# Chunks summed and rounded in pairs, x_lo on GpSimd, y kept in PSUM: a conditioned FFN in split fp32

## What is computed

```python
q_emb = relu(cond @ W3 + b3)                     # one row of 512 per batch
v_sum = sum(x, axis=1, keepdims=True)            # over the 64 tokens of a batch
x1 = (64 * x + v_sum) * q_emb[:, None, :]
y = relu(x1 @ W2 + b2)
base = y @ W_base + b_base
shared = (y @ A_s) @ B_s                         # rank 16
gates = softmax(y @ W_router + b_router)         # 6 experts, the top 2 are kept
routed = sum over e of ((y @ A_r[e]) * w[e]) @ B_r[e]  # w: kept gates, not renormalised
out = x + base + shared + routed
```

## Time and profile before

| | |
|---|---|
| time, median of 3 | 252.19 us |
| the three runs | 253.6, 252.19, 251.87 us |
| span of the profiled execution | 249.2 us |
| mean granted clock of TensorE | 0.979 of full speed |
| TensorE busy | 234.5 us (94%), 999 matmuls |
| VectorE busy | 205.4 us (82%), 396 instructions |
| ScalarE busy | 90.8 us (36%), 170 instructions |
| GpSimd busy | 54.8 us (22%), 52 instructions |
| DMA | 28.47 MB, mean 114 GB/s |

### The profile page before, as it was taken

How to read it: one execution, slowest core, us unless ns; L and a number is a source line. 1 busy time by engine, 2 the same in 40 slices (tenths; PEclk the granted TensorE clock), 3 DMA queues, 4 the chain that set the end, 5 groups by cost and what they waited for, 6 DMA issues and landing times.

```text
span 249.2 us, 3161 instructions
## 1 busy us (share of the span) xinstructions
PE 234.5 (94%) x999; PEld 186.3 (75%) x999; DVE 205.4 (82%) x396; ACT 90.8 (36%) x170; POOL 54.8 (22%) x52
## 2 busy tenths in 40 slices
PE   6699799699998988999999999999999999999994
PEld 2488568478786766888888888888888888888863
DVE  0697999979998998989988997989798997752384
...
GB/s 157 291 203 208 261 231 2 170 0 291 50 3 166 0 259 187 61 1 180 194 134 0 60 277 166 6 0 257 80 0 0 168 169 0 0 60 109 3 0 168
DMA packets 32217, 28.47 MB, mean 114 GB/s; under 512 B 6173, under 2 KB 22621, under 8 KB 32206
## 3 DMA queue, kind: packets, MB, share of 16 engines
...
...
HBM read 19.94 MB, written 8.39 MB: 114 GB/s over the span
## 4 chain that ended last, share of the span: by engine, by line
PE 56%; DVE 27%; SPq 6%; DMA 4%; issue 4%; ACT 2%; POOL 1%; POOLq 0%; DVEq 0%; ACTq 0%
PE m_ps L630 51%; PE hT L630 6%; DVE xT L388 5%; DMA x_quart<-in_x_dram 4%; DVE gatesT L488 4%; DVE vsum L393 3%; DVE x_sum L402 3%; DVE x_lo L410 3%; DVE y_lo L416 3%; DVE out_nat L513 2%; SPq L212 2%; SPq L200 1%; DVE hw_full L497 1%; DVE logit L448 1%; SPq L206 1%
## 5 line engine op out<-in xcount | busy, mean ns | idle before, releaser
L267 POOL TENSOR_TENSOR x_full<-x_sum,qT 128x512 f32<-128x512 f32 x31 | 38.1, 1230 | 141.6 <-DVE x_sum L402 141.6
L630 PE MATMUL m_ps<-Wb_hi,y_hi 128*128 128x512 f32 x128 | 49.9, 390 | 0.0
L630 PE MATMUL m_ps<-Wb_lo,y_hi 128*128 128x512 f32 x128 | 49.8, 389 | 0.0
L630 PE MATMUL m_ps<-Wb_hi,y_lo 128*128 128x512 f32 x128 | 49.8, 389 | 0.0
L630 PE MATMUL m_ps<-x_hi,W_hi 128*128 128x512 f32 x112 | 44.1, 394 | 4.1 <-DVE x_lo L410 2.9
L630 PE MATMUL m_ps<-x_lo,W_hi 128*128 128x512 f32 x112 | 43.7, 390 | 0.0
L630 PE MATMUL m_ps<-x_hi,W_lo 128*128 128x512 f32 x112 | 43.6, 389 | 0.0
L388 DVE STREAM_TRANSPOSE xT<-x_quart 128x512 f32<-128x512 f32 x32 | 35.0, 1093 | 6.9 <-DMA x_quart<-in_x_dram 6.9
L312 ACT ACTIVATE y_full<-m_ps,b_sb 128x512 f32<-128x512 f32 x32 | 22.0, 688 | 40.3 <-PE m_ps L630 37.4
L304 ACT ACTIVATE x_hi<-x_full 128x512 fp32r<-128x512 f32 x32 | 20.0, 629 | 35.8 <-POOL x_full L267 35.8
L488 DVE STREAM_TRANSPOSE gatesT<-w_nat 32x128 f32<-32x128 f32 x96 | 29.1, 303 | 3.0
...
## 6 DMA issues: line engine op xcount, KB each, us to landing
...
```

Of the source, the lines that this page charges most:

```text
L267: nc.gpsimd.tensor_tensor(per_batch(x1_full[:, c, :]), per_batch(x1_sum[:, c, :]), qT[:, c, bass.ds(BG * g, BG)].unsqueeze(2).to_broadcast ...
L630: mm = nc.tensor.matmul(psum, lhsT, rhs, start=start and i == 0, stop=stop and i == len(terms) - 1)
```

## The change

- `xT` and `vsum` hold two chunks. From group 1 on, `sum_x` and `add_sum` work on a pair of chunks in one instruction (1,024 columns), and `x1_split` rounds a pair in one. `scale` still works on one chunk. Group 0 goes by single chunks (`sum_first`, `add_first`, `rest_first`).
- From group 1 on, x1_lo is made by GpSimd (`x1_rest`), after the pair was rounded, in the order scale, scale, rest, rest for each pair. TensorE also waits for x1_hi.
- ScalarE makes y_hi first and then writes relu over the bank of m1 itself; y_full is gone, and with it the wait for y_lo ahead of the relu. VectorE's `y_rest` takes y from PSUM.
- The orders on VectorE and ScalarE are rewritten accordingly; both transposes of a pair come together, and the 12 gate transposes are in one piece in all groups but the last.

```diff
-        xT = [sb(f"xT{i}", [P, TG]) for i in range(2)]
+        xT = [sb(f"xT{i}", [P, 2, TG]) for i in range(2)]
         out_nat = [sb(f"out_nat{i}", [P, TT, D]) for i in range(2)]
-        vsum = [sb(f"vsum{i}", [P, BG]) for i in range(2)]
+        vsum = [sb(f"vsum{i}", [P, 2, BG]) for i in range(2)]
         x1_sum = sb("x1_sum", [P, KC, TG])
         x1_full = sb("x1_full", [P, KC, TG])
         x1_hi = [sb(f"x1_hi{i}", [P, KC, TG], F32R) for i in range(2)]
         x1_lo = [sb(f"x1_lo{i}", [P, KC, TG], F32R) for i in range(2)]
-        y_full = [sb(f"y_full{i}", [P, TG]) for i in range(2)]
         y_hi = sb("y_hi", [P, KC, TG], F32R)
...
+
+        def pairs_done(g, j):
+
+            return KC + PAIRS * (g - 1) + j + 1
...
-                pool.wait_ge(x1_sum_ready, n + 1)
-
-                if not (isinstance(g, int) and g == 0):
+                if isinstance(g, int) and g == 0:
+                    pool.wait_ge(x1_sum_ready, c + 1)
+                else:
+                    pool.wait_ge(x1_sum_ready, pairs_done(g, c // 2))
                     pool.wait_ge(x1_lo_ready, n + 1 - KC)
                 nc.gpsimd.tensor_tensor(per_batch(x1_full[:, c, :]), per_batch(x1_sum[:, c, :]),
                                         qT[:, c, bass.ds(BG * g, BG)].unsqueeze(2).to_broadcast([P, BG, N]),
                                         ALU.mult).then_inc(x1_full_ready, 1)
+
+            def x1_rest(g, par, c):
+
+                pool.wait_ge(x1_hi_ready, pairs_done(g, c // 2))
+                nc.gpsimd.tensor_tensor(x1_lo[par][:, c, :], x1_full[:, c, :],
+                                        x1_hi[par][:, c, :].bitcast(F32), ALU.subtract).then_inc(x1_lo_ready, 1)
 
             def W_rest(lo, full, hi, n, ready):
 
@@ -281,14 +293,20 @@
             W_rest(Wd_lo[:, :, :], Wd_f[:, :, :], Wd_hi[:, :, :], KC + 1, Wd_lo_ready)
             for k in range(KC):
                 W_rest(Wb_lo[:, k, :], Wb_f[:, k, :], Wb_hi[:, k, :], KC + 2 + k, Wb_lo_ready)
-            scale(1, 0)
-            scale(1, 1)
-            W_rest(Wu_lo[:, :], Wu_f[:, :], Wu_hi[:, :], 2 * KC + 2, Wu_lo_ready)
-            for c in range(2, KC):
-                scale(1, c)
-            with pool.Fori(2, NG) as g:
-                for c in range(KC):
-                    scale(g, c)
+            def prepare(g, par, between=None):
+
+                for j in range(PAIRS):
+                    scale(g, 2 * j)
+                    scale(g, 2 * j + 1)
+                    if j == 0 and between is not None:
+                        between()
+                    x1_rest(g, par, 2 * j)
+                    x1_rest(g, par, 2 * j + 1)
+
+            prepare(1, 1, lambda: W_rest(Wu_lo[:, :], Wu_f[:, :], Wu_hi[:, :], 2 * KC + 2, Wu_lo_ready))
+            with pool.Fori(0, (NG - 2) // 2) as pair:
+                for half in range(2):
+                    prepare(pair * 2 + (2 + half), half)
 
         @block.scalar
...
-            def x1_split(g, par, c):
-
-                act.wait_ge(x1_full_ready, KC * g + c + 1)
-                nc.scalar.activation(x1_hi[par][:, c, :], x1_full[:, c, :], ACT.Copy).then_inc(x1_hi_ready, 1)
-
-            def relu(g, m, first):
+            def x1_split(g, par, c, n=1):
+
+                act.wait_ge(x1_full_ready, KC * g + c + n)
+                nc.scalar.activation(x1_hi[par][:, c:c + n, :], x1_full[:, c:c + n, :], ACT.Copy).then_inc(x1_hi_ready, 1)
+
+            def relu(g, m):
 
                 n = KC * g + m
                 act.wait_ge(m1_done, n + 1)
-                if not (first and m < 2):
-                    act.wait_ge(y_lo_ready, n - 1)
-                nc.scalar.activation(y_full[m % 2][:, :], m1_ps[m][:, :], ACT.Relu,
-                                     bias=b2_sb[:, m:m + 1]).then_inc(y_full_ready, 1)
                 nc.scalar.activation(y_hi[:, m, :], m1_ps[m][:, :], ACT.Relu,
                                      bias=b2_sb[:, m:m + 1]).then_inc(y_hi_ready, 1)
+                nc.scalar.activation(m1_ps[m][:, :], m1_ps[m][:, :], ACT.Relu,
+                                     bias=b2_sb[:, m:m + 1]).then_inc(y_full_ready, 1)
 
             act.wait_ge(condT_done, 1)
             nc.scalar.activation(condT[:, :, :], hT[:, 0:QC * B].rearrange("p (k b) -> p k b", b=B), ACT.Copy).then_inc(condT_copied, 1)
...
-                def split(c):
+                def split(j):
                     if not last:
-                        x1_split(g + 1, 1 - par, c)
+                        x1_split(g + 1, 1 - par, 2 * j, 2)
 
                 for m in range(KC):
-                    relu(g, m, first)
-                    if not first and m >= (2 if second else 1):
-                        split(m - (2 if second else 1))
+                    relu(g, m)
+                    if not first and m == (3 if second else 1):
+                        split(0)
                 if first:
                     act.wait_ge(Wu_loaded, 48)
                     nc.scalar.activation(Wu_hi[:, :], Wu_f[:, :], ACT.Copy).then_inc(W_hi_ready, 1)
@@ -361,14 +377,9 @@
                 nc.scalar.activation(h_sb[:, :], hT[:, :], ACT.Identity, bias=h_bias[:, 0:1]).then_inc(h_ready, 1)
                 if first:
                     split(0)
-                    split(1)
-                if second:
-                    split(2)
                 act.wait_ge(logit_ready, g + 1)
                 nc.scalar.activation(expo[:, :, :], logit[:, :, :], ACT.Exp).then_inc(expo_ready, 1)
-                if first:
-                    split(2)
-                split(3)
+                split(1)
                 parts = 2 if last else 1
                 for i in range(parts):
                     toks = slice(i * TG // parts, (i + 1) * TG // parts)
...
-                nc.vector.transpose(xT[c % 2][:, :], x_quart[par][:, :, :].rearrange("p b (i c) -> p c b i", c=KC)[:, c]).then_inc(xT_ready, 1)
-
-            def sum_x(g, c):
-
-                dve.wait_ge(xT_ready, KC * g + c + 1)
-                nc.vector.tensor_reduce(vsum[c % 2][:, :], per_batch(xT[c % 2][:, :]), AX.X,
+                nc.vector.transpose(xT[c // 2][:, c % 2, :], x_quart[par][:, :, :].rearrange("p b (i c) -> p c b i", c=KC)[:, c]).then_inc(xT_ready, 1)
+
+            def per_pair(ap):
+                return ap.rearrange("p c (b n) -> p (c b) n", n=N)
+
+            def sum_x(g, j):
+
+                dve.wait_ge(xT_ready, KC * g + 2 * j + 2)
+                nc.vector.tensor_reduce(vsum[j][:, :, :].rearrange("p c b -> p (c b)"), per_pair(xT[j][:, :, :]), AX.X,
                                         ALU.add).then_inc(vsum_ready, 1)
 
-            def add_sum(g, c):
-
-                n = KC * g + c
-                dve.wait_ge(vsum_ready, n + 1)
-                if not (isinstance(g, int) and g == 0):
-                    dve.wait_ge(x1_full_ready, n + 1 - KC)
+            def add_sum(g, j):
+
+                dve.wait_ge(vsum_ready, pairs_done(g, j))
+                dve.wait_ge(x1_full_ready, KC * g + 2 * j + 2 - KC)
                 nc.vector.scalar_tensor_tensor(
-                    out=per_batch(x1_sum[:, c, :]), in0=per_batch(xT[c % 2][:, :]), scalar=float(N),
-                    in1=vsum[c % 2][:, :].unsqueeze(2).to_broadcast([P, BG, N]),
+                    out=per_pair(x1_sum[:, 2 * j:2 * j + 2, :]), in0=per_pair(xT[j][:, :, :]), scalar=float(N),
+                    in1=vsum[j][:, :, :].rearrange("p c b -> p (c b)").unsqueeze(2).to_broadcast([P, 2 * BG, N]),
                     op0=ALU.mult, op1=ALU.add).then_inc(x1_sum_ready, 1)
 
-            def x1_rest(g, par, c):
-
-                dve.wait_ge(x1_hi_ready, KC * g + c + 1)
-                nc.vector.tensor_tensor(x1_lo[par][:, c, :], x1_full[:, c, :],
-                                        x1_hi[par][:, c, :].bitcast(F32), ALU.subtract).then_inc(x1_lo_ready, 1)
+            def sum_first(c):
+
+                dve.wait_ge(xT_ready, c + 1)
...
-                dve.wait_ge(y_hi_ready, KC * g + m + 1)
-                nc.vector.tensor_tensor(y_lo[:, m, :], y_full[m % 2][:, :],
+                dve.wait_ge(y_full_ready, KC * g + m + 1)
+                nc.vector.tensor_tensor(y_lo[:, m, :], m1_ps[m][:, :],
                                         y_hi[:, m, :].bitcast(F32), ALU.subtract).then_inc(y_lo_ready, 1)
 
 
             turn_x(0, 0, 0)
-            sum_x(0, 0)
...
-                def total(*chunks):
-                    for c in () if last else chunks:
-                        sum_x(g + 1, c)
-                        add_sum(g + 1, c)
-
-                def rest(*chunks):
-                    for c in () if last else chunks:
-                        x1_rest(g + 1, 1 - par, c)
+                def sums(j):
+                    if not last:
+                        sum_x(g + 1, j)
+
+                def adds(j):
+                    if not last:
+                        add_sum(g + 1, j)
 
                 if first:
-                    turn(0)
-                    total(0)
+                    turn(0, 1)
```

(94 more changed lines are left out.)

## The result

The changed kernel takes 256.16 us (median of 4 runs, 255.37 to 256.73), against 252.03 (median of 4) before: ratio 1.017, 95% interval 1.012 to 1.022. It is slower by 4.1 us. I had forecast 253.5, in a range from 251.0 to 257.0, with 0.57 on a change within 1% and 0.36 on slower. So the likeliest class did not come; the sign of the sum (+1.3) and the range held, and two thirds of the size was missed.

What follows compares the result with a forecast made beforehand. TensorE was taken to bound the kernel, losing time only in groups 0 to 2. Span 249.2 + 1.3 = 250.5, the loop adding 0 to 0.1 per group; with 3.0 between span and median, 253.5 us, range 251.0 to 257.0.

Steps and rivals of the forecast that it cites:

- the sum (+1.3): Group 2's last y_lo product at 97.45 against 96.11, so the span grows by 1.3 us; the loop adds 0 to 0.1 per group.
- (a): Loop, groups 3 to 6: turns to VectorE's pace, m1's last column tile waiting for out_nat; 255.5 us; chance 0.23.
- (b): y_lo from PSUM is blocked by GpSimd all the same; group 0's last y_lo product at 35.75, not 33.05; 256.2 us; chance 0.10.
- x_lo at 1.59 us: Upper bound for one x_lo on GpSimd, against 1.29 taken; six in the two chains, +1.8 us.
- TensorE sets the pace; only groups 0 to 2 matter: Groups 3 to 7 follow at TensorE's pace, 27.20 us; its lost time is seven waits in groups 0 to 2, 6.61 us.
- Prices: Estimated instruction times: 1024-column pair 1.23 us on VectorE, 1.06 on ScalarE; x_lo on GpSimd 1.29; y_lo from PSUM at most 0.69.
- Group 0: Group 0's y_lo products start at 28.16 to 33.05, the last having stood at 35.18: 2.13 us earlier.
- no y_lo wait over 0.2: Sign that the walk is right: TensorE has no y_lo wait of over 0.2 us in group 0.
- The chains of groups 1 and 2: Scalings, pair split and x_lo delay chunk 3's first product: 49.76 against 49.22 in group 1, 81.94 against 77.94 in group 2.
- Rival (c): GpSimd's chain is not late, so no product waits and all of 6.6 us goes: 245.6 us; chance 0.07.
- 68 products (15.4 us) and 0.1 for a restart lead to 97.45: Group 2: from chunk 3's product at 81.94, TensorE reaches the last y_lo product at 97.45, against 96.11.
- Rival (d): VectorE's pairs cost as much as two singles: +0.6 us, 254.1; chance 0.56 together with the main walk.

Runs made afterwards that it cites:

- e1_warm: Changed kernel, with TensorE running 16 products of a zero tile in groups 1 and 2 during the wait for chunk 2's x_lo: 252.45 us, ratio 1.002.
- e5_single: Changed kernel's y in PSUM and x_lo on GpSimd, but every chunk summed, scaled and rounded singly in the earlier kernel's order: 248.03 us, ratio 0.983.
- e4_psum: Kernel before plus one part of the change alone: y_hi first, relu over the bank, y_lo from PSUM: 249.13 us, ratio 0.990.

## Why the prediction was right or wrong

**The range held by luck.** Its upper part was made of (a), (b) and x_lo at 1.59 us, and none of these came; what filled it was a term that the sum did not have.

**TensorE sets the pace; only groups 0 to 2 matter: right.** The loop's groups take 27.20 us in both kernels and the rest after 100.98 is unchanged.

**Prices: right.** The groups of the changed kernel (busy, mean ns of one, idle before):

```profile
L280 POOL TENSOR_TENSOR x_lo<-x_full,x_hi 128x512 fp32r<-128x512 f32 x28 | 36.4, 1320 | 19.3 <-ACT x_hi L322 19.3
...
L442 DVE TENSOR_TENSOR y_lo<-m_ps,y_hi 128x512 fp32r<-128x512 f32 x32 | 21.8, 684 | 13.5 <-ACT m_ps L330 13.5
...
L330 ACT ACTIVATE m_ps<-m_ps,b_sb 128x512 f32<-128x512 f32 x32 | 20.9, 655 | 0.0
...
L407 DVE TENSOR_REDUCE vsum<-xT 128x16 f32<-128x1024 f32 x14 | 17.1, 1219 | 0.4
...
L322 ACT ACTIVATE x_hi<-x_full 128x1024 fp32r<-128x1024 f32 x14 | 14.8, 1054 | 35.4 <-POOL x_full L273 35.4
```

x_lo on GpSimd 1.32 us (1.29 taken), the pair sum 1.22 (1.23), the pair's rounding 1.05 (1.06), y_lo from PSUM 0.684, the relu into PSUM 0.655. The 62 cycles more for a PSUM source that the Trainium skill, VectorE: DVE Perf Modes, the errata section, charges do not appear: y_lo is no slower than the 0.693 of the SBUF form.

**y_lo from PSUM is not blocked, x_sum is: right,** rival (b) out. GpSimd's Wb_lo against two instructions of VectorE:

```profile
25.48 6.01 POOL L286 TENSOR_TENSOR Wb_lo<-Wb_f,Wb_hi 128x512 fp32r<-128x512 f32 x4
...
26.31 0.69 DVE L442 TENSOR_TENSOR y_lo<-m_ps,y_hi 128x512 fp32r<-128x512 f32 x1
...
28.64 1.72 DVE L414 SCALAR_TENSOR_TENSOR x_sum<-xT,vsum 128x1024 f32<-128x1024 f32 x1
```

At 26.31, inside GpSimd's row, y_lo takes 0.69; at 28.64 the pair addition takes 1.72 instead of 1.23. The rule of the Trainium skill, SBUF — State Buffer, Who interferes with whom, that an instruction of VectorE with at most one SBUF input does not contend, holds here for this form.

**Group 0: right in the main.** The last y_lo product is at 32.52. Its first h product came 0.9 us earlier than before by itself (26.82 against 27.70), so 1.8 of the gain are the change's, against 2.13 forecast. The sign that no y_lo wait over 0.2 would be left in group 0 was not met: 0.56 at 31.01. And the size is not firm: in e1_warm, with the same code up to there and the first h product at 26.81, the last y_lo product stands at 33.75.

**The chains of groups 1 and 2: right.** I had chunk 3 of group 1 16.71 us after the last y_lo product of group 0 (33.05 to 49.76); it was 16.42. Group 2's chain in the trace, VectorE, GpSimd and ScalarE:

```profile
69.61 0.31 DVE L470 STREAM_TRANSPOSE h_nat<-h_head 128x128 f32<-128x128 f32 x1 [3.24 <-ACT h_head L373]
...
75.48 1.23 DVE L414 SCALAR_TENSOR_TENSOR x_sum<-xT,vsum 128x1024 f32<-128x1024 f32 x1
...
76.97 2.04 POOL L273 TENSOR_TENSOR x_full<-x_sum,qT 128x512 f32<-128x512 f32 x2 [6.16 <-DVE x_sum L414]
...
79.04 1.06 ACT L322 ACTIVATE x_hi<-x_full 128x1024 fp32r<-128x1024 f32 x1 [7.94 <-POOL x_full L273]
...
80.18 2.95 POOL L280 TENSOR_TENSOR x_lo<-x_full,x_hi 128x512 fp32r<-128x512 f32 x2 [1.17 <-ACT x_hi L322]
...
80.76 1.23 DVE L523 TENSOR_TENSOR hw_full<-h_sb,gatesT 128x512 f32<-128x512 f32 x1
```

From h_nat (68.27 walked, 69.61 here) through the pair addition, two scalings, the pair's rounding and x_lo(2), each piece ends 1.3 to 1.4 us later than walked, as the chain starts 1.3 later, so each lasts what I gave it. hw_full is blocked as foreseen (1.23 instead of 0.69). Rival (c) is out: nothing came early.

**Where it failed: "68 products (15.4 us) and 0.1 for a restart lead to 97.45".** This took the full clock for granted after a wait of 4 us, in group 2 and, unsaid, in group 1 as well. From 48.94 and from 83.18 on, the next eleven steps take 4.86 and 4.84 us instead of 2.49, nearly all of them 0.43 instead of 0.23 us; less the 0.1 that I had for a restart, that is 4.6 us in all. 97.45 - 0.9 + 4.6 = 101.15, and 100.98 was measured. I had read the clock row only for the loop, although the stretch before TensorE has steady work had shown a lower clock there too (0.81 of full speed in the first 12 us), and I had not counted rivals of this kind at all. e1_warm shows the term by itself: the two stretches are 2.3 us shorter each once the clock is held up.

**The loop, rival (a): not met,** by as little as walked. The same stage, beside the earlier trace rows:

```profile
132.23 2.53 POOL L280 TENSOR_TENSOR x_lo<-x_full,x_hi 128x512 fp32r<-128x512 f32 x2 [1.66 <-ACT x_hi L322]
...
132.50 1.07 DVE L501 SCALAR_TENSOR_TENSOR expo_top<-rank,expo 128x24 f32<-128x24 f32 x1
...
133.68 1.50 DVE L505 TENSOR_TENSOR w_nat<-expo_top,rden 128x384 f32<-128x384 f32 x1
...
140.62 0.69 DVE L528 TENSOR_TENSOR hw_lo<-hw_full,hw_hi 128x512 fp32r<-128x512 f32 x1 [0.70 <-ACT hw_hi L387]
...
147.37 1.88 DVE L539 TENSOR_TENSOR out_nat<-m_ps,x_nat 128x512 f32<-128x512 f32 x3
```

x_lo(2) starts 0.27 us ahead of expo_top and blocks it and then w_nat (1.07 and 1.50 us), just as worked out. From hw_lo at 140.62 to the end of the second out_nat at 147.37 + 1.29 = 148.66 it is 8.0 us (8.1 given). TensorE did not wait.

**Rival (d): not met**; two singles would be 1.38, a pair is 1.22.

Why pairs are worse than singles is shown in part. In the changed kernel chunk 2 must wait for chunk 3's transpose, which in groups 0 and 1 stands behind the gates, and so one late chunk becomes two; e5_single, which takes this apart, gains 8.1 us (5.5 between the two profiled runs, 4.6 of these behind chunk 3 of group 1). In group 1 single chunks with x_lo on GpSimd have a hole as long (3.95 us), where y in PSUM alone has 1.67 (e4_psum, at 47.99). Pairs with the old order of VectorE were not run, and how the 8.1 us divide into lateness and clock was not measured by a run of its own.
